# Causal attention with ALiBi on one core: score units in pairs on ScalarE, low parts in place, an order for each engine

## The reference

```python
xn = layernorm(x)
q, k, v = (proj(W, b) for W, b in ...)            # 16 heads of 32
scores = q @ k.T / sqrt(32) + slope[h] * (j - (s - 1))   # j: key
scores = where(causal, scores, min)
ctx = softmax(scores) @ v;  attn = ctx @ Wo + bo
ffn = mixture of 8 experts, the best 2 of each token, silu(g) * u, F = 256 each
out = x + attn + ffn
```

## Time and profile before

| | us |
|---|---|
| median of 3 runs | 1972.61 (1968.24 to 1977.61) |
| profiled execution: span from the first to the last instruction | 1970.9 |
| TensorE busy in the span | 1897.6 (96%) |
| VectorE, ScalarE, GpSimd busy | 1501.2, 1400.8, 1372.3 |
| heads, about 340 to 1447 us of the span | 1107 |
| last head, then output projection and experts | 1447 to 1971 |

### The profile page before, as it was taken

One profiled execution on the slowest core, in us unless ns is written; L12 is line 12 of the kernel. 1 busy time (PEld: TensorE's weight loads), 2 busy tenths in 40 slices (PEclk: granted clock), 3 DMA queues, 4 the chain that ended last, 5 costly groups with the idle time before them and its releaser, 6 DMA issues. The chain is left out here.

```text
span 1970.9 us, 39142 instructions
## 1 busy us (share of the span) xinstructions
PE 1897.6 (96%) x8656; PEld 1425.0 (72%) x8657; DVE 1501.2 (76%) x3466; ACT 1400.8 (71%) x2728; POOL 1372.3 (70%) x1183
## 2 busy tenths in 40 slices
PE   6999999999999999999999999999998989999997
PEld 5787777676767777777677776776756767887876
DVE  6454566888989989899899898898966965666654
ACT  4333322998999989999999899998973335555554
POOL 4111113898988989889889898898948846666664
PEclk9999999999999999999999999999999999999998
DMA  8577758242242432423324224243226766656554
GB/s 268 193 260 258 272 179 283 75 114 64 73 104 61 97 80 63 113 62 81 96 62 108 69 71 106 61 96 81 62 72 183 252 197 118 104 103 104 104 99 66
DMA packets 119241, 242.13 MB, mean 123 GB/s; under 512 B 17632, under 2 KB 54368, under 8 KB 112896
## 3 DMA queue, kind: packets, MB, share of 16 engines
q1 hardware_dynamic: 101120, 205.84, 36.0%
q0 software_dynamic: 18080, 35.81, 10.3%
HBM read 139.28 MB, written 104.21 MB: 124 GB/s over the span
## 5 line engine op out<-in xcount | busy, mean ns | idle before, releaser
L1173 POOL TENSOR_TENSOR probs_lo<-probs,probs_hi 128x512 fp32r<-128x512 f32 x781 | 984.1, 1291 | 158.6 <-ACT probs L1208 156.7
L1207 ACT ACTIVATE probs_hi<-s_ps 128x512 fp32r<-128x512 f32 x905 | 602.0, 665 | 84.3 <-DVE s_ps L1280 80.2
L1208 ACT ACTIVATE probs<-s_ps 128x512 f32<-128x512 f32 x964 | 613.3, 670 | 9.8 <-DVE s_ps L1280 6.4
L1259 DVE TENSOR_REDUCE m_part<-m_ps 128x1 f32<-128x512 f32 x744 | 491.1, 685 | 9.5 <-PE m_ps L1500 5.9
L1516 PE MATMUL s_ps<-q_st,k_st 100*128 100x512 f32 (+3 forms) x880 | 327.9, 413 | 16.5 <-ACT probs L1208 11.8
L1500 PE MATMUL m_ps<-k_st,q_st 98*128 98x512 f32 (+2 forms) x840 | 282.0, 377 | 0.3 <-DVE m_part L1256 0.3
L1535 PE MATMUL o_ps<-probs_hi,v_split 128*96 128x512 f32 (+3 forms) x720 | 266.8, 380 | 1.7 <-POOL probs_lo L1173 1.7
L1536 PE MATMUL o_ps<-probs_lo,v_split 128*96 128x512 f32 (+3 forms) x720 | 259.2, 363 | 0.0
L1256 DVE CUSTOM_DVE_ANT_0 m_ps<-m_ps,mask_row 128x128 f32<-128x128 f32 x496 | 242.0, 498 | 22.5 <-PE m_ps L1500 16.3
L1516 PEld LDWEIGHTS s_ps<-q_st,k_st 100*128 100x128 f32 x880 | 161.5, 190 | 103.0 <-ACT probs L1208 37.9
L621 POOL TENSOR_TENSOR v_rows<-v_raw,v_rows 128x512 fp32r<-128x512 f32 x32 | 41.2, 1291 | 229.4 <-ACT v_rows L677 229.4
(11 more groups left out here) (236 smaller groups left out, 3658.2 us busy)
## 6 DMA issues: line engine op xcount, KB each, us to landing
v_d<-v_rows SPq DMA_DIRECT2D x7, 3072.0 KB, 9.4
v_split<-v_d SPq DMA_DIRECT2D x22, 768.0 KB, 8.5
k_st<-k_hi_d SPq DMA_DIRECT2D x44, 256.0 KB
q_st<-q_hi_d SPq DMA_DIRECT2D x44, 256.0 KB
xn_d<-xs SPq DMA_DIRECT2D x8, 1024.0 KB, 11.7
q_hi_d<-qk_hi SPq DMA_DIRECT2D x32, 256.0 KB, 8.0
q_lo_d<-qk_lo SPq DMA_DIRECT2D x32, 256.0 KB, 7.9
k_hi_d<-qk_hi SPq DMA_DIRECT2D x32, 256.0 KB, 3.5
```

Source lines behind the costliest of these rows:

```text
L1173: nc.gpsimd.tensor_tensor(*low_operands(u), ALU.subtract).then_inc(lo_ready_pool, 1)
L1207: nc.scalar.activation(probs_hi[:, P_SLOT[u]], scores, ACT.Exp, scale=SCALE)
L1208: nc.scalar.activation(scores if kind == "Q" else probs[:, P_SLOT[u]], scores, ACT.Exp, scale=SCALE).then_inc(p_ready, 1)
L1259: V.tensor_reduce(top, scores, AX.X, ALU.max).then_inc(m_taken, 1)
```

## The change

- KIND becomes 26 P, 7 D and 1 W. D replaces Q: ScalarE writes the full exponential to SBUF as for P, and VectorE subtracts there.
- probs_lo is laid on probs (same addresses): GpSimd and VectorE subtract in place. The ring of slots grows from nine to twelve.
- Score units go in 18 groups (GROUPS): unit 0 alone, 16 pairs, unit 33 alone. ScalarE reads two neighbouring banks, 128 x 1024, and writes two neighbouring slots; p_ready counts groups. A pair starts when both units are scored and masked. s_ps has four banks, m_ps two.
- One order for each engine in place of one for all, with lags of its own.
- The last head's order is built from these; one wait is added there before the banks of m_ps are used again (counts_taken).

```diff
-KIND = "PPWPPPPPPWPPPPQPPPWPPQPQPPWPPWQPPP"
+KIND = "WPPPPPDPPPPDPDPPPPPPPPDPPDPPDDPPPP"
-ORDER = ("SMMMVVVMVMMVLSSMVMLLSMVMMVOVSLMSMVSLSMLMLVSMSMVSLMLMLVMMOVSMSSVMMSVMVMDOSLMVLLSVSMVSVMSMVSMMVSMVMSLD"
-         "LVSLMLLVMDLSMVSMMSSVMSVLSVXWVSLVLLDSOVSVLLS")
-BACK = {'V': 8, 'L': 4, 'O': 1}
+ORDERS = {"PE": ("MVMVMVMVSMSMVSMSSMVVMVMVMSMSSMSMVMVSMSMVVSMSMVMVMSSVMMVSSMVMSSVMVMSSMVVMMSSVMVMVSSMMVSSMVMVSMSMVVMSM"
+              "SVVSSWVVS"),
+          "ACT": ("EEEOEEEOEEEOEEEEEEEEOE"),
+          "DVE": ("MMDMMSMMSOMSMMMMMSMSMMOMMDMMMMOMMDMMSSMMMSDMMMMOMMMMDMMMMXDSWDS"),
+          "POOL": ("LLLLLLLLLLLLLLLLLLLLLLLLLL"),}
+BACK = {("PE", "V"): 9, ("ACT", "O"): 1, ("DVE", "D"): 1, ("DVE", "O"): 2, ("POOL", "L"): 2}
-P_RING = 9
+P_RING = 12
-M_BUFS, S_BUFS = 3, 3
+M_BUFS, S_BUFS = 2, 4
+GROUPS = [range(0, 1), range(1, 3), range(3, 5), ..., range(31, 33), range(33, 34)]
...
+        probs_at = nc.sbuf_base
         probs = sb(ctx, "probs", [P, P_RING, CH], F32)
+        probs_lo = nc.alloc_sbuf_tensor_at("probs_lo", [P, P_RING, CH], F32R, offset=probs_at)
         probs_hi = sb(ctx, "probs_hi", [P, P_RING, CH], F32R)
-        probs_lo = sb(ctx, "probs_lo", [P, P_RING, CH], F32R)
...
+            def weights(n, g):
+                units, kind = GROUPS[g], kinds(n)
+                first, last = units[0], units[-1]
+                act.wait_ge(s_ready, NS * n + last + 1)
+                if any(s_diagonals(u) for u in units):
+                    act.wait_ge(s_masked, masked_count(n, last))
+                act.wait_ge(pv_done, PV_START + NS * n + max(u - units_between(u) for u in units) + 1)
+                split = [u for u in units if kind[u] != "W"]
+                if split:
+                    nc.scalar.activation(probs_hi[:, P_SLOT[split[0]]:P_SLOT[split[0]] + len(split)],
+                                         s_ps[:, S_BANK[split[0]]:S_BANK[split[0]] + len(split)], ACT.Exp, scale=SCALE)
+                nc.scalar.activation(probs[:, P_SLOT[first]:P_SLOT[first] + len(units)],
+                                     s_ps[:, S_BANK[first]:S_BANK[first] + len(units)], ACT.Exp,
                                      scale=SCALE).then_inc(p_ready, 1)
...
             def low_part(n, u):
-                dve.wait_ge(p_ready, NS * n + u + 1)
-                V.tensor_tensor(probs_lo[:, P_SLOT[u]], s_ps[:, S_BANK[u]], probs_hi[:, P_SLOT[u]].bitcast(F32),
-                                ALU.subtract).then_inc(lo_ready_dve, 1)
+                dve.wait_ge(p_ready, NG * n + GROUP[u] + 1)
+                V.tensor_tensor(*low_operands(u), ALU.subtract).then_inc(lo_ready_dve, 1)
```

More of the change, by code:

```diff
@@ L128 @@
+BACK = {("PE", "V"): 9, ("ACT", "O"): 1, ("DVE", "D"): 1, ("DVE", "O"): 2, ("POOL", "L"): 2}
 HEADS_RING = 3
-P_RING = 9
+P_RING = 12
 LAST_WHOLE = [u for u in range(NS) if u not in (21, 23, 25, 27, 29, 30)]
-P_SLOT = [*range(8), *range(9), *range(8), *range(9)]
+P_SLOT = [0, 2, 3, 4, 5, 6, 7, 8, 9, 10, 11, 0, 1, 2, 3, 4, 5, 6, 7, 8, 9, 10, 11, 0, 1, 2, 3, 4, 5, 6, 7, 8, 9, 10]
 assert len(P_SLOT) == NS
-M_BUFS, S_BUFS = 3, 3
[L136 to L143, removed]
+M_BUFS, S_BUFS = 2, 4
@@ new lines, with attend_order @@
+S_BANK = [0, 2, 3, 0, 1, 2, 3, 0, 1, 2, 3, 0, 1, 2, 3, 0, 1, 2, 3, 0, 1, 2, 3, 0, 1, 2, 3, 0, 1, 2, 3, 0, 1, 2]
+GROUPS = [range(0, 1), range(1, 3), range(3, 5), range(5, 7), range(7, 9), range(9, 11), range(11, 13), range(13, 15), range(15, 17), range(17, 19), range(19, 21), range(21, 23), range(23, 25), range(25, 27), range(27, 29), range(29, 31), range(31, 33), range(33, 34)]
+NG = len(GROUPS)
+GROUP = [g for g, units in enumerate(GROUPS) for _ in units]
+def attend_order(engine):
+    units = {"S": [u for u in range(NS) if engine != "DVE" or s_diagonals(u)], "M": list(range(NM)), "V": list(range(NS)),
+             "E": list(range(NG)), "X": [0], "W": [0], "L": [u for u in range(NS) if KIND[u] == "P"],
+             "D": [u for u in range(NS) if KIND[u] == "D"], "O": list(range(S // CH))}
@@ L144, in attend_order @@
     order, seen = [], collections.Counter()
-    for kind in ORDER:
-        at = seen[kind] - BACK.get(kind, 0)
+    for kind in ORDERS[engine]:
+        at = seen[kind] - BACK.get((engine, kind), 0)
         order.append((kind, units[kind][at], int(at < 0)))
         seen[kind] += 1
-    assert all(seen[kind] == len(units[kind]) for kind in units)
+    assert all(seen[kind] == len(units[kind]) for kind in seen)
     return order
-ATTEND = attend_order()
+ATTEND = {engine: attend_order(engine) for engine in ORDERS}
@@ L159, in last_order @@
 def last_order():
[L161 to L164, removed]
+    waiting = {k: sorted({(k, u, 1) for order in ATTEND.values() for kind, u, back in order if kind == k and back})
+               for k in "VLDO"}
+    due = [*range(3 - len(waiting["O"]), 3)] + [u + LAST_LAG + 3 for u in LAST_UNIT]
     waiting["V"] += [("V", u, 0) for u in range(NS)]
@@ L167, in last_order @@
     waiting["O"] += [("O", u, 0) for u in range(S // CH)]
-    due = [2] + [u + LAST_LAG + 3 for u in LAST_UNIT]
-    order, late = [], BACK["V"]
+    order = waiting["D"]
     for u in range(NS + LAST_LAG + 4):
@@ L172, in last_order @@
             order.append(("S", u, 0))
+            if u == GROUPS[GROUP[u]][-1]:
+                order.append(("E", GROUP[u], 0))
         while waiting["L"] and (waiting["L"][0][2] or waiting["L"][0][1] < u):
@@ L184, in last_order @@
             due.pop(0)
-    assert not any(waiting.values())
+    assert not any(waiting[kind] for kind in "VLO")
     return order
-LAST_ATTEND = last_order()
+LAST_ORDER = last_order()
+LAST_ATTEND = {engine: [token for token in LAST_ORDER if not token[2] or token in ATTEND[engine]] for engine in ORDERS}
 LOOPS = (NH - 2) // HEADS_RING
@@ L1049, in attend @@
         counted = sem(ctx, "counted")
+        counts_taken = sem(ctx, "counts_taken")
         gap_ready = sem(ctx, "gap_ready")
@@ L1098, in step_n @@
                 maxima = not is_last(n)
-                for kind, u, back in ATTEND if maxima else LAST_ATTEND:
+                for kind, u, back in (ATTEND if maxima else LAST_ATTEND)["DVE"]:
                     if kind == "O" and (before or not back):
@@ L1225, in step_n @@
             def step_n(n, before=True):
-                for kind, u, back in LAST_ATTEND if is_last(n) else ATTEND:
-                    if kind == "S":
+                for kind, u, back in (LAST_ATTEND if is_last(n) else ATTEND)["ACT"]:
+                    if kind == "E":
                         weights(n, u)
@@ L1336, in place_tokens @@
                 step.settle()
+                dve.sem_inc(counts_taken, 1)
                 for e in range(E):
@@ L1555, in spread_first @@
                 pe.wait_ge(spread_ready, 1)
+                pe.wait_ge(counts_taken, 1)
                 for g in range(G):
@@ L1566, in step_n @@
                     pe.wait_ge(st_loaded[r1], 16 * ST_DMAS * st_round)
-                for kind, u, back in ATTEND if maxima else LAST_ATTEND:
+                for kind, u, back in (ATTEND if maxima else LAST_ATTEND)["PE"]:
                     if not maxima and (kind, u) == ("S", 9):
```

26 lines of the change are left out of this document (6 added, 20 removed).

## The result

The changed kernel takes 2477.22 us (2467.79 to 2491.88, 4 runs) against 1970.89 before: ratio 1.257, interval 1.252 to 1.262. Slower, as forecast; but by 506 us, not 58, far outside the range. The span of the profiled execution is 2480.1 us.

A forecast was written before the change was run, and what follows sets the result against it. VectorE was to become the bound: 33.2 us of work, 7 x 0.45 for the D and 1.1 of waits make 37.5 us a head against 35.7. Times 31 heads, +56 us: 2029 us, range 1975 to 2110.

The forecast's parts named there:

- VectorE's sum of work bounds a head: VectorE per head: 33.2 us of work plus 7 x 0.45 is 36.4; with 1.1 of waits, 37.5 us.
- over 96%: Sign in the profile after: VectorE is busy over 96% in a head, TensorE under 92%.
- rival (C): Delays behind each D travel through TensorE's banks and ScalarE's masks: 40.0 us a head, 2106 us (2060 to 2150); chance 0.19.
- the spread of the D: Sign: a D lasts 0.69 plus 0.2 to 0.8 us on average, widely spread, where Q had 681 to 694 ns.
- GpSimd's second duration: Sign: GpSimd's subtractions have two durations, 1.29 and about 1.75 us, seven of the longer a head.
- the price of a D on VectorE: Each D loses what is left of one GpSimd subtraction, less 0.14: 0.45 us, between 0 and 1.12.
- 3.8 us of air in a head take that up: TensorE, only two tiles ahead with two maxima banks, stands soon after a D; its 3.8 us of air absorb that.
- TensorE's longest wait: Reading of the kernel before: 13.3 us in 28 heads, so TensorE's order leaves no gap to speak of.
- In place: GpSimd's subtractions in place or not cost the same: two reads, one write.
- Pairs: ScalarE's exponentials of 1024 columns cost 0.90 us each, from above 0.96; ScalarE 32.2 us a head, or 34.1.
- A W less on TensorE: Four W fewer (5 to 1) save 4 x 0.39 = 1.5 us of TensorE's 35.2 a head, leaving 33.7.

The follow-up runs named there:

- e5: Kernel before with two PSUM banks for the maxima instead of three: 2131 us, ratio 1.080.
- e16: Changed kernel with SyncE's loads one O earlier and the transpose of maxima two score units earlier, no seams on GpSimd: 2410 us, ratio 1.222.
- e9: Changed kernel with GpSimd waiting for its own last subtraction, loads one O earlier and the transpose two score units earlier: 2096 us, ratio 1.062.
- e11: Kernel before with low parts laid on probs and a ring of twelve slots instead of nine: 1974 us, ratio 1.000.
- e15: Kernel before with low parts in place, ring of twelve, and ScalarE taking units two and one in turn from three banks: 2307 us, ratio 1.171.
- e12: Kernel before with low parts in place, ring of twelve, and unit 9 split instead of whole (4 W): 1987 us, ratio 1.008.
- e6: Structure of the change (pairs, four score banks, two maxima banks) with the order and kinds of the kernel before: 2349 us, ratio 1.190.
- e2: Changed kernel with the D set earlier in VectorE's order, still reading both operands from SBUF, in pairs: 2342 us, ratio 1.185.
- e4: Changed kernel with GpSimd waiting for the end of its own subtraction before starting the next: 2240 us, ratio 1.136.
- e1: Changed kernel with D reading the full exponential from PSUM, groups with a D taken unit by unit, D earlier in VectorE's order: 2268 us, ratio 1.150.

## Why the prediction was wrong

**Direction: right. Mechanism: right in part.** That seven subtractions with both operands in SBUF and GpSimd's hold each other off, and that VectorE becomes the busiest engine, both came true. That VectorE's sum of work bounds a head is not: it is busy 85%, not over 96%, and waits 7.9 us in a head, where I had 1.1. That is rival (C), the delays travel, beyond the price I gave it (2106, at most 2150). Of the signs I named, the spread of the D is there (668 to 6144 ns). GpSimd's second duration is there too, 1.71 to 1.76 us where I had 1.75, but on 26 of its 451 subtractions, the ones before which a D got in, not on seven a head.

**The step that failed: the price of a D on VectorE, "the loss is what is left, less 0.14", 0.45 us.** Measured: 2.16 - 0.69 = 1.47. The rule itself holds for all D that get in at the first end of a GpSimd instruction: at 1099.23 some 0.42 us were left, and the D lost 0.28. What it leaves out is that GpSimd's next subtraction can go first. The rows I had were of GpSimd instructions behind which none came close; I carried them over to a queue that starts each instruction before the last has ended. There 27 of 121 D stood for the rest of one instruction and four whole ones, and lost 5.35 us each, 81% of all that VectorE lost; the other 94 lost 0.36 on average, near my 0.45. The prediction had this half a sentence long inside rival (C) ("GpSimd's next subtraction goes ahead of a waiting D") and gave it no price; seven times a run of three to five instructions would have been 26 to 44 us a head as a bound from above, where my bound was 1.12 us a D.

The Trainium skill's rule, whoever is first holds the ports for its whole instruction ("SBUF — State Buffer", Who interferes with whom), agrees with the 60 D that waited for one instruction. It does not tell of the 27: there GpSimd kept VectorE out for up to four further instructions.

VectorE's busy time fits the measured duration, 28.9 + 7 x 2.16 = 44.0 us against 44.6; the head's 52.45 does not follow from it.

**Two readings of mine.** I gave 13.3 us as TensorE's longest wait. Its weight loads, which I left out, waited longer, 39.7 us in 900 for ScalarE to free a bank of scores; so TensorE was less clearly the bound than I wrote. And I took the Q out of VectorE's sum with their duration, 0.69, and put the D in with their distance, 0.61: with the distance for both its sum is 0.3 us higher. The second decides nothing here.

**"3.8 us of air in a head take that up": wrong.** In the kernel before, two maxima banks alone cost 5.2 us a head (e5). As I read it, air spread over a head does not help a wait that recurs at tile after tile. I had bounded this edit by no row.

**Not seen at all: the end of a head.** The change moves the transpose towards the end, and with VectorE's O also the loads that SyncE issues. I costed neither: each instruction in the moved step, its DMAs above all, had to be followed. Worth 67 to 144 us (e16, e9).

**TensorE's clock** was taken as 1.00. It is 0.85 in the stretch: after each long stand it is 0.50 for some microseconds, and products then lie 0.43 us apart instead of 0.235. This makes each stand dearer than itself.

**The terms at nothing or in favour.** In place: right (e11). Pairs: their own time was right, 0.91 us from start to start where 0.90 was taken, but what they ask of the banks was not in the sum (e15). A W less on TensorE: 0.39 in the rows, and yet no gain (e12); TensorE's busy time in a head is 35.6 us there against 35.2, and busy shares of 98.5% and 93% on two engines do not say which paces.

**What remains open.** Why a D gets in at the first end in one head and stands in another; the 125 us by which e9 is still behind, of which e5, e6 and e15 show possible causes only in the old order; and what paces the kernel before. No variant tried beats the kernel before.

## What to carry to other kernels

When two engines can hold each other off, ask not only how long one instruction is but also how long the other's queue runs without a gap, and give the case that it keeps going first a price of its own; a wait of an engine for its own last instruction can be the cheapest way to let the other in. When work is taken off the engine that looks busiest, first check by one small edit that it paces the loop. And when an order is rewritten, follow what hangs on each letter, the DMA issues of the queue that walks along included.

## What the runs showed that was not expected

- A VectorE subtraction with two SBUF operands that meets overlapping subtractions of GpSimd either gets in at the first end or waits out the whole run. It got in 26 times of 53 in the changed kernel and 76 of 84 in e2; it stood 27 times in the changed kernel, up to 6.1 us. With the extra wait of e4 it took at most 1.52 us. It ends 0.55 us after the GpSimd instruction it waited for. With one operand in PSUM it takes 0.68 to 0.69 us whatever GpSimd does (e1, and the earlier trace rows).
- In this contest GpSimd loses little: its mean rises from 1291 to 1315 ns without seams, to 1368 with them. An instruction before which VectorE got in takes 1.71 to 1.76 us.
- After stands of TensorE of 4.58 us (e1) and 4.82 us (the changed kernel) its granted clock was 0.50 in the windows of 4 and 6 us that followed.
